# Reordering the prologue of a hybrid convolution, attention and expert kernel

## The reference

```python
A = -exp(log_A_real) + 1j * A_imag            # [H=128, N=64]
dt = exp(log_dt)[:, None];  dtA = dt * A
Ct = (C_re + 1j * C_im) * (exp(dtA) - 1.0) / A
V = exp(dtA[:, :, None] * l[None, None, :])   # l = 0..255
K = 2.0 * real(einsum('hn,hnl->hl', Ct, V))   # the filter, 128 x 256
y = irfft(rfft(x, 512) * rfft(K, 512).T, 512)[:, :256, :]
r = x + y + x * D
out = (r - mean(r)) * rsqrt(var(r) + 1e-5) * ln_w + ln_b
```

## Time and profile before

| What | Value |
|---|---|
| time, median of 3 runs | 901.4 us (901.35 to 901.77) |
| span of the profiled execution | 899.3 us, from its first to its last instruction |
| busy in that span: PE, DVE, ACT, POOL | 70%, 71%, 49%, 51% |
| stretch before PE's first matmul | 40.9 us |
| stretch from there to POOL's first sending of rows | 40.9 to 137.2 us |

### The profile page before, as it was taken

The page is one execution under the profiler, slowest core; times in us unless marked ns, Lnnn a source line. Parts: engine busy times, 40 slices in busy tenths (PEclk is TensorE's granted clock), DMA queues, the critical chain, the costliest instruction groups (busy, mean ns, idle before and its releaser), DMA issues. The chain is left out here.

```text
span 899.3 us, 21979 instructions
## 1 busy us (share of the span) xinstructions
PE 633.2 (70%) x7826; PEld 468.5 (52%) x7826; DVE 635.0 (71%) x1395; ACT 445.1 (49%) x873; POOL 456.7 (51%) x569
## 2 busy tenths in 40 slices
PE   0197973882059999324799998998963795999950
PEld 0073432562049999312566665665641564998850
DVE  6989988681048888387677777877741972888855
ACT  5632167670035555271766665665642242555534
POOL 1126767887637777510002222554573881677760
PEclk9978997896579999755899999999985997999985
DMA  9510001432134563242121322332111412454418
GB/s 287 132 37 1 0 0 45 83 80 58 44 60 90 102 93 84 85 162 60 45 83 50 91 73 73 78 105 74 49 36 37 80 34 48 84 97 93 93 27 281
DMA packets 131850, 70.51 MB, mean 78 GB/s; under 512 B 89535, under 2 KB 118725, under 8 KB 131746
## 3 DMA queue, kind: packets, MB, share of 16 engines
q1 hardware_dynamic: 121042, 50.46, 23.8%
q0 software_dynamic: 9088, 16.88, 6.9%
q10 hardware_dynamic: 1616, 1.77, 0.7%
HBM read 26.61 MB, written 30.50 MB: 64 GB/s over the span
## 5 line engine op out<-in xcount | busy, mean ns | idle before, releaser
L1437 ACT ACTIVATE ARENA<-banks,ARENA 128x256 f32<-128x256 f32 x312 | 122.2, 474 | 104.2 <-PE banks L1400 86.7
L2150 DVE TENSOR_REDUCE ARENA<-banks 128x4 f32<-128x1024 f32 (+1 forms) x128 | 122.7, 959 | 46.7 <-PE banks L1891 45.4
L1398 PE MATMUL banks<-ARENA,W1H 128*128 128x256 f16 x312 | 87.1, 279 | 65.3 <-DMA ARENA<-slots 58.2
L2072 ACT ACTIVATE ARENA<-banks 128x1536 f32<-128x1536 f32 x64 | 92.8, 1450 | 58.2 <-PE banks L1919 58.2
L1412 PE MATMUL banks<-W2L,ARENA 128*128 x624 | 110.8, 220 | 3.2 <-DVE ARENA L1450 2.4
L1414 PE MATMUL banks<-W2H,ARENA 128*128 x624 | 110.2, 219 | 0.0
L1413 PE MATMUL banks<-W2H,ARENA 128*128 x624 | 110.1, 219 | 0.0
L1388 POOL DMA_INDIRECT expert_out_g<-ARENA x78 | 80.6, 1034 | 47.7 <-issue 25.8
L1388 POOL DMA_INDIRECT expert_out_f<-ARENA x78 | 80.0, 1026 | 37.5 <-issue 25.8
L1471 DVE TENSOR_TENSOR ARENA<-ARENA 128x1024 f16<-128x1024 f32 x78 | 95.6, 1226 | 2.7
L1000 POOL DMA_INDIRECT slots<-ARENA,PLACE x64 | 77.6, 1212 | 28.4 <-issue 20.4
(11 more groups left out here) (312 smaller groups left out, 1812.0 us busy)
## 6 DMA issues: line engine op xcount, KB each, us to landing
spread<-ARENA SPq DMA_DIRECT2D x96, 64.0 KB, 2.1
ARENA<-expert_out_f SPq DMA_DIRECT2D x8, 512.0 KB, 7.4
ARENA<-spread SPq DMA_DIRECT2D x16, 256.0 KB, 3.0
ARENA<-spread SPq DMA_DIRECT2D x32, 128.0 KB, 3.0
ARENA<-expert_out_g SPq DMA_DIRECT2D x8, 512.0 KB, 7.3
XT<-in_w SPq DMA_DIRECT2D x10, 256.0 KB, 7.7
slots<-EMPTY SPq DMA_DIRECT2D x16, 129.0 KB, 4.5
ARENA<-in_w SPq DMA_DIRECT2D x8, 256.0 KB, 6.8
```

The costliest lines, as they stand in the source:

```text
L1398: pe.matmul(out, t.W1H[:, e, ms], XST[i][:, 0], start=True, stop=False)
L1437: ins = nc.scalar.activation(HF[i % 2][:, m], UP[i % 2][:, m], ACT.Gelu, bias=BIAS[i % 4][:, m:m + 1], scale=1.0 / WS)
L2072: nc.scalar.activation(PR[x % 2], t.psum_all[:, 5:8, :], ACT.Exp, scale=1.0 / LOGIT).then_inc(exps, 1)
L2150: dve.tensor_reduce(MX[:, G // 2, tile, :, :, G % 2].rearrange("p s a -> p a s"), src, AX.X, ALU.max).then_inc(m_red, 1)
```

## The change

The edits lie in the lists of SP, POOL, ACT, PE and DVE of `front_stage`.

- ACT begins with one exponential of one element (GATE, of which nothing reads this word), behind a wait for POOL's third memset, then the two exponentials, and issues the second half of x only after them. The other four transfers go to SP's list, behind the first eight weights.
- The 16 phases SINA are made by ACT (Identity with a scale and a bias), between MAG2 and MAG1, and announced by a new semaphore `lines_ready`; DVE keeps `turn_rest`.
- DVE's first `x_statistics` comes after the phases of one step instead of before.
- On ACT the absolute value stays ahead of the first `normalise`, the two last sines come after it, and the first six `split_high`, which stood before them, join the others.
- SIN2 times MAG2 goes from POOL to DVE. `add_shift(0)` moves up to between `root_x(0)` and `root_x(1)`.
- The four products of 128x2048 are each made in two halves along the channels; `e1_ready` is raised after each half, and PE waits for the second before channel 64.
- On DVE, `split_low` of the first 16 jobs is cut differently: 4, 4, 4, 4 instead of 3, 7, 2, 4. The copy for `kch_sb` and `x_statistics(2)` come before the scaling of B2; `x_offsets(2)` goes between the first two `products`, and `split_low` of 8 to 11 behind them.

```diff
@@ SP
             for i in range(NS // 2):
                 load(i)
+            sp.dma_start(t.ID, ...).then_inc(dct_in, 16)
+            sp.dma_start(IV, ...).then_inc(ln_in, 16)
+            sp.dma_start(WLN, ...).then_inc(ln_in, 16)
+            sp.dma_start(DCOL, ...).then_inc(ln_in, 16)
@@ POOL
             root_x(0)
-            pool.wait_ge(mags, 1)
-            pool.wait_ge(sines, 1)
-            nc.gpsimd.tensor_tensor(SIN2, SIN2, MAG2, ALU.mult).then_inc(e2_ready, 1)
+            add_shift(0)
             root_x(1)
-            add_shift(0)
             root_x(2)
             add_shift(1)
@@ ACT
-            act.dma_start(t.RES[:, NT // 2:, :], ...).then_inc(x_in, 16)
-            act.dma_start(t.ID, ...); (IV, ...); (WLN, ...); (DCOL, ...)
+            act.wait_ge(pool_step, 1)
+            nc.scalar.activation(t.GATE[0:1, 0:1], t.MHALF[0:1, 0:1], ACT.Exp)
             act.wait_ge(params_in, 32)
             nc.scalar.activation(PRM[:, DT, :], PRM[:, LDT, :], ACT.Exp)
             nc.scalar.activation(PRM[:, LAR, :], PRM[:, LAR, :], ACT.Exp).then_inc(exps, 1)
+            act.dma_start(t.RES[:, NT // 2:, :], ...).then_inc(x_in, 16)
...
+            act.wait_ge(steps_ready, 1)
+            for a in range(LF):
+                ins = nc.scalar.activation(SINA[:, a, :], TMP[:, 2, :], ACT.Identity, bias=OFF[:, 1:2], scale=float(a))
+            ins.then_inc(lines_ready, 1)
             for a in range(LF):
                 ins = nc.scalar.activation(MAG1[:, a, :], TMP[:, 0, :], ACT.Exp, scale=-float(LF * a))
...
-            split_high(range(0, 6))
-            act.wait_ge(phase_ready, 3)
-            nc.scalar.activation(SINB, SINA, ACT.Abs).then_inc(folded, 1)
-            act.wait_ge(folded, 1)
-            (the two sines of SINA and SINB)
...
+            act.wait_ge(phase_ready, 3)
+            nc.scalar.activation(SINB, SINA, ACT.Abs).then_inc(folded, 1)
             normalise(0)
+            act.wait_ge(folded, 1)
+            (the two sines of SINA and SINB)
             act.wait_ge(dct_in, 48)
             nc.scalar.activation(t.ID16, t.ID, ACT.Copy)
-            split_high(range(6, NS))
+            split_high(range(0, NS))
@@ PE
             for h in range(D):
+                if h == D // 2:
+                    pe.wait_ge(e1_ready, 2)
@@ DVE
             turn_rest(SIN2, KQ).then_inc(phase_ready, 1)
-            dve.wait_ge(x_in, 32)
-            x_statistics(0)
             (phases of one step, turn_rest, phase_ready 2)
-            for a in range(LF):
-                ins = ts(SINA[:, a, :], R16, float(a), OFF[:, 1:2], ALU.mult, ALU.add)
-            link(ins)
+            dve.wait_ge(x_in, 32)
+            x_statistics(0)
+            dve.wait_ge(lines_ready, 1)
             turn_rest(SINA, PHR).then_inc(phase_ready, 1)
             x_offsets(0)
             (coefficients)
+            tt_(SIN2, SIN2, MAG2, ALU.mult).then_inc(e2_ready, 1)
             dve.wait_ge(sines, 3)
             dve.wait_ge(mags, 2)
-            (four products of 128x2048)
+            for h in range(2):
+                a, b = halved(SINA, h), halved(SINB, h)
+                tt_(a, a, along(CTR, h), ALU.mult)
+                dve.wait_ge(sines, 4)
+                link(tt_(b, b, along(CTI, h), ALU.mult))
+                link(tt_(a, a, b, ALU.add))
+                tt_(a, a, halved(MAG1, h), ALU.mult).then_inc(e1_ready, 1)
             x_statistics(1)
-            split_low(range(0, 3))
+            split_low(range(0, 4))
             x_offsets(1)
-            split_low(range(3, 10))
+            split_low(range(4, 8))
+            (wait kch_mm, the copy for kch_sb)
+            x_statistics(2)
             (wait small, scaling of B2, memsets)
-            (wait kch_mm, the copy for kch_sb)
-            x_statistics(2)
-            split_low(range(10, 12))
-            x_offsets(2)
             dve.wait_ge(kf_mm, 1)
...
             products(0, 0)
+            x_offsets(2)
             products(0, 1)
+            split_low(range(8, 12))
             x_statistics(3)
             split_low(range(12, 16))
             x_offsets(3)
```

More of the change, by code:

```diff
@@ L194, in front_stage @@
         empty_row, emptied, fixed, small = sem("empty_row"), sem("emptied"), sem("fixed"), sem("small")
-        steps_ready, folded = sem("steps_ready"), sem("folded")
+        steps_ready, folded, lines_ready = sem("steps_ready"), sem("folded"), sem("lines_ready")
         jobs = weight_jobs(t)
@@ L232, in _ @@
                 load(i)
+            sp.dma_start(t.ID, t.dram["ident"]).then_inc(dct_in, 16)
+            sp.dma_start(IV, t.dram["inv"].rearrange("t p f -> p t f")).then_inc(ln_in, 16)
+            sp.dma_start(WLN, t.dram["ln"].rearrange("k p h -> p k h")).then_inc(ln_in, 16)
+            sp.dma_start(DCOL, t.dram["dcol"]).then_inc(ln_in, 16)
             for v, name in ((t.B1, "b1"), (t.B2, "b2_rows"), (t.GB[:, 0, :], "gate_b"), (t.GB[:, 1, :], "rank"),
@@ L367, in _ @@
             nc.scalar.activation(PRM[:, LAR, :], PRM[:, LAR, :], ACT.Exp).then_inc(exps, 1)
+            act.dma_start(t.RES[:, NT // 2:, :], t.dram["x"].rearrange("b (t p) d -> p (b t) d", p=P)[:, NT // 2:, :]).then_inc(x_in, 16)
             act.wait_ge(decay_ready, 1)
@@ L385, in _ @@
             nc.scalar.activation(TMP[:, 4:6, :], TMP[:, 4:6, :], ACT.Sin, scale=TURN).then_inc(sines, 1)
-            split_high(range(0, 6))
-            act.wait_ge(phase_ready, 3)
-            nc.scalar.activation(SINB, SINA, ACT.Abs).then_inc(folded, 1)
-            act.wait_ge(folded, 1)
-            nc.scalar.activation(SINA, SINA, ACT.Sin, scale=TURN).then_inc(sines, 1)
-            nc.scalar.activation(SINB, SINB, ACT.Sin, bias=OFF[:, 3:4], scale=-TURN).then_inc(sines, 1)
             m_n = rows_of(t.NRM, 0, NT)
@@ L432, in gelu @@
                 nc.scalar.activation(H16[:, g % 2, 0], HF[:, g % 2], ACT.Copy).then_inc(high, 1)
+            act.wait_ge(phase_ready, 3)
+            nc.scalar.activation(SINB, SINA, ACT.Abs).then_inc(folded, 1)
             normalise(0)
+            act.wait_ge(folded, 1)
+            nc.scalar.activation(SINA, SINA, ACT.Sin, scale=TURN).then_inc(sines, 1)
+            nc.scalar.activation(SINB, SINB, ACT.Sin, bias=OFF[:, 3:4], scale=-TURN).then_inc(sines, 1)
             act.wait_ge(dct_in, 48)
             nc.scalar.activation(t.ID16, t.ID, ACT.Copy)
-            split_high(range(6, NS))
+            split_high(range(0, NS))
             for q in range(4):
@@ L673, in _, with halved, along @@
             link(tt_(CTI, CTI, INV, ALU.mult))
+            tt_(SIN2, SIN2, MAG2, ALU.mult).then_inc(e2_ready, 1)
             dve.wait_ge(sines, 3)
             dve.wait_ge(mags, 2)
[L677 to L681, removed]
+            def halved(v, h):
+                return v[:, :, D // 2 * h:D // 2 * (h + 1)]
+            def along(v, h):
+                return v[:, D // 2 * h:D // 2 * (h + 1)].rearrange("p (o h) -> p o h", o=1).broadcast_to([P, LF, D // 2])
+            for h in range(2):
[5 more added lines that the diff above has]
+                tt_(a, a, halved(MAG1, h), ALU.mult).then_inc(e1_ready, 1)
             x_statistics(1)
-            split_low(range(0, 3))
+            split_low(range(0, 4))
             x_offsets(1)
-            split_low(range(3, 10))
+            split_low(range(4, 8))
+            dve.wait_ge(kch_mm, 1)
+            dve.wait_ge(ln_in, 48)
+            link(dve.tensor_copy(KCH.rearrange("p (a b) -> p b a", b=LF), ps[4][:, 0:SEQ].rearrange("p (b a) -> p b a", a=LF)))
+            ts(KCH[:, 0:1], KCH[:, 0:1], DCOL, 1.0, ALU.add, ALU.add).then_inc(kch_sb, 1)
+            x_statistics(2)
             dve.wait_ge(small, 96)
```

## The result

The changed kernel takes 891.5 us (median of 4 runs, 890.4 to 893.9) against 901.4 us (4 runs, 899.7 to 901.8): a ratio of 0.989, 95% interval 0.987 to 0.991, 9.9 us less. The forecast was 890.4 in a range of 887.5 to 894.5, and faster. The execution that was profiled is the slowest of the four (span 892.2 us), so its end is not compared with that of before; its landmarks are.

| landmark | before, us | forecast | after, us |
|---|---|---|---|
| ACT's first exponential | 7.23 | 4.7 | 4.23 |
| DVE's first instruction | 7.78 | 5.3 | 4.77 |
| `x_offsets(0)`, right behind the phases of SINA | 31.83 | z' + 16.5 | 21.22 = z' + 16.45 |
| PE's first matmul | 40.92 | z' + 21.9 | 26.47 = z' + 21.7 |
| the channels' end | 60.03 | z' + 41.6 | 46.37 = z' + 41.6 |

What follows compares the result with a forecast made beforehand. Bound: one-engine-at-a-time chain in the prologue, then DVE in the convolution, up to POOL's first send. 2.5 + 10.65 - 2.1 = 11.0 us takes the span from 899.3 to 888.3; plus 2.1, median 890.4, range 887.5 to 894.5.

Steps and rivals of the forecast that it cites:

- z': The time of DVE's first instruction in the new kernel, from which the forecast counts; forecast at 5.3 us.
- Two exponentials first: Head of ACT: exponentials at 4.7 us, waiting only for parameters and offsets; gain 2.5 us, bounds 0.7 to 3.3.
- The rival that they are slow by themselves: Head: small pieces are slow even alone, exponentials at 6.5 us; gain 0.7 instead of 2.5, time 892.2; chance 0.13.
- The wait for x: Before DVE's statistics: second half of x, issued later, lands at z'+9.6 with 0.9 us of slack and costs nothing.
- The rival with the uneven share: Second half of x gets 26% of packets, lands at z'+16.2, 5.6 us late; 890.4 to 896.0; chance 0.14.
- Phases on ACT: Prologue: DVE loses 7.55 us of SINA phases; the 3.25 us added on ACT are hidden by 2.3 us.
- The norm: Prologue on ACT: norm starts before the two last sines, 3.7 us off PE's start, which moves to z'+21.9.
- The coefficients: DVE before the channels: `add_shift(0)` stops an instruction, coefficients end at 24.7 instead of z'+22.4; PE waits 0.6 us.
- The convolution gives back: DVE's new order in the convolution: -1.9 + 0.1 + 2.4 + 2.4 - 0.9 = 2.1 us later; bounds -1.9 to +4.
- The sum: Whole change: 2.5 + 10.65 - 2.1 = 11.0 us off the span, 899.3 to 888.3.

## Why the prediction was right

- **Two exponentials first**, 2.5 us forecast, 3.0 measured (7.78 to 4.77), within its bounds of 0.7 to 3.3. The mechanism is the one given: with x away from the queues the small packets were through by 3.75 us rather than the 4.5 of the forecast, and with x first 2.05 of the 3.0 are gone. The rival that they are slow by themselves falls.
- **The wait for x** cost nothing, as forecast, but with less room than it said. The first packets came some 4.2 us after the issue instead of 2.5: 52 by 9 us. From 9 to 13 us x then got 408 packets to SP's 457, 102 and 114 a us. By packets that is nearly one to one. It agrees with the turns, a packet each, that the Trainium skill gives (DMA: Bandwidth & Descriptors, "Queues, rings and completion order"). By bytes it is not the half that the forecast took: 0.82 MB to 0.44, for x 205 GB/s instead of 147. The forecast had x land at z' + 9.6, and it landed between z' + 9.7 and 10.0 (526 of its 528 packets by 14.5 us, all by 14.75). That is partly luck: the forecast had the start 1.7 us too early and the rate 58 GB/s too low, and the two cancel. Some 0.5 us of slack was left of 0.9; one of the experiments overdrew it by 0.42. The rival with the uneven share, 5.6 late, falls.
- **Phases on ACT**, 7.55 forecast: `x_offsets(0)` at z' + 16.45 against 16.5. The size is right; the split is what the forecast left open, 3.2 for the move and 4.3 for POOL's product that no longer stands beside it. ACT's part was priced too low, 3.25 instead of 4.79. The 0.093 us more in each of the sixteen agree with what the Trainium skill (ScalarE: Activation LUTs, "What ACT_TABLE_LOAD costs") gives for an operand taken by a pointer. No table is loaded between the exponentials and these lines.
- **The norm**, 3.7: undoing it moves PE's start by 3.9 (30.34 against 26.47). **The coefficients**: POOL stopped L673 for the whole of its add, and PE waited 0.66 against 0.6. The channels end at z' + 41.6, the forecast to the tenth.
- **The convolution gives back**, 2.1 forecast, 2.76 measured at the first send. To `products(1, 0)` it is 2.0 (24.86 to 26.86), and there the sum holds term by term: the spectrum is taken up 1.8 earlier (1.9 forecast), the four `split_low` with POOL's stops take 4.62 (4.8), and L80's stop of 0.9 is gone. To the inverse at 110.05 it is 2.0 as well (121.70 less 60.03, 110.05 less 46.37). The other 0.75 arises there: those 8 matmuls took 5.09 us, at a granted clock of 0.72, where they took 3.71 in the kernel before, at 1.00, and DVE waits 1.74 for what follows (L961). That price was not in the sum. What the sum cannot say is whose price the 2.0 is: the forecast set it down to the new order with `split_low`, but with the old order `products(1, 0)` comes later still (27.56). DVE's work in that stretch is what does not shrink, and moving eight `split_low` out of it is worth 5.5 us at the first send.
- **The sum** was 11.0, and 10.90 was kept to the end of the first expert stage: half a microsecond more at the head, 0.7 less in the convolution. That the two offset each other is luck. The 2.1 us that it added to the span were a slip: they set the span of the profiled execution against the median of three runs, and in every later run span and time are 1.7 to 1.8 apart (892.2 and 893.88), which takes some 0.3 to 0.4 off. The median lies 1.1 us above the forecast as given, and no profile shows the median's own execution. In the profiled one 3.8 us are lost behind the first expert stage: 2.6 in the two waits for the experts' rows and 1.1 in the rest of the attention.
- **What stays open** is why the attention takes 386.6 to 390.5 us in profiles whose program there is the same. The clock in the stretch shown above goes with it at the ends (0.76 and 386.7 in the kernel before, 0.76 and 386.6 with `add_shift` late, 0.67 and 389.0 in the changed one, 0.59 and 390.5), but one run had 0.62 and 387.4. The wait for the experts' rows at its start is a part: 15.6 to 16.0 us in five of the twelve profiles, 16.9 to 17.2 in the others. What sets the clock there, or that wait, was not tried.

## What to carry to other kernels

Issue what the first instruction waits for before anything large, on the other queues too: small pieces that shared the engines with a large transfer came 2 us later than alone. When a chain ahead of a busy engine is cut, ask which work of that engine stood in the old waits; it has to move with the cut, and here moving eight instructions of it (`split_low`) brought 4.4 us on top of the change's 9.9, though four of the eight then overran their new pause by 1.4. Follow a gain by landmarks to the end of the kernel, since behind the first send these runs differed by more than some of the edits were worth.

## What was not expected of the hardware

- The same eight matmuls (the inverse released by POOL after a pause of 3.1 us on PE) took 3.71 us in the kernel before, 5.09 in the changed one and 6.76 with the sines first, at granted clocks of 1.00, 0.72 and 0.54. The pause before them was the same to 0.01 us, so the last pause does not tell at which level the clock stands. The next inverse took 5.37 in the kernels before and after, behind pauses of 1.36 and 0.73, and 3.68 in three experiments, behind 0.72 to 0.73.
- POOL's adds stop DVE's instructions with two operands in SBUF (0.68 became 1.75, 0.29 became 2.44), which agrees with the Trainium skill (SBUF — State Buffer, "Who interferes with whom"). By that rule POOL's root (L283, two operands in SBUF, 2.03 us from 68.75) would have to stop `split_low` too; the row at 69.18 took 0.69. The measurement decides here: an instruction of POOL of 8 elements a partition did not hold DVE up through its span, and spans on POOL are rough.
- One tensor operand can be enough. The line of SINA that POOL's product held up (L643, 4.61 us instead of 0.28) reads one tensor and a column of offsets.
- A transfer issued while the other queue was busy began some 4.2 us after its issue, where the one issued at 0.86 began after about 2.5.
